# A lead of four tiles and a mean turned by transposing DMA, in a graph, attention and expert layer on one core

## What is computed

```python
deg = max(segment_sum(ones, dst), 1)
xn = layernorm(x)
agg = segment_sum(xn[src], dst) / deg[:, None]          # the mean over incoming edges
x = x + xn @ W1.T + b1 + agg @ W2.T + b2                # graph part
      + attention(xn)                                   # linear attention, 16 heads
x = x + experts(layernorm(x))                           # two chosen experts of eight
```

## Time and profile before

| | us |
|---|---|
| median of 3 executions | 1580.96 (1580.53 to 1581.2) |
| the profiled execution | 1580.07 |
| its span, first to last instruction | 1578.3 |
| TensorE busy | 1519.8 (96%) |
| VectorE, ScalarE, GpSimd busy | 1003.1, 604.5, 799.0 |
| first pass | up to about 325 |
| layers | about 350 to 1295 |
| experts | behind that |

### The profile page before, as it was taken

The page is one execution under the profiler, slowest core; times in us unless marked ns, Lnnn a source line. Parts: engine busy times, 40 slices in busy tenths (PEclk is TensorE's granted clock), DMA queues, the critical chain, the costliest instruction groups (busy, mean ns, idle before and its releaser), DMA issues.

```text
span 1578.3 us, 29172 instructions
## 1 busy us (share of the span) xinstructions
PE 1519.8 (96%) x7597; PEld 733.7 (46%) x7598; DVE 1003.1 (64%) x2154; ACT 604.5 (38%) x997; POOL 799.0 (51%) x847
## 2 busy tenths in 40 slices
PE   5999999989999999999999999999999989999997
PEld 2444444444544444444444444444544444444443
DVE  7576522246666667666677666666666666666777
ACT  5777721111333333332333333333333335555554
POOL 4122143646777767777767777767777710000000
PEclk8999999999999999999999999999999989999998
DMA  9977776957777767777767777767777723322323
GB/s 237 262 170 190 189 179 132 217 151 208 234 235 234 234 209 231 234 234 237 233 206 239 239 240 233 234 209 236 236 233 233 233 80 120 107 90 96 106 87 112
DMA packets 166610, 308.64 MB, mean 196 GB/s; under 512 B 71986, under 2 KB 74572, under 8 KB 166260
## 3 DMA queue, kind: packets, MB, share of 16 engines
q0 software_dynamic: 62720, 205.57, 44.3%
q1 hardware_dynamic: 36112, 58.90, 11.7%
q10 hardware_dynamic: 67684, 42.96, 10.7%
HBM read 255.02 MB, written 39.49 MB: 187 GB/s over the span
## 4 chain that ended last, share of the span: by engine, by line
PE 70%; POOL 14%; issue 6%; DVE 3%; DMA 1%; ACT 0%; DVEq 0%; SPq 0%; ACTq 0%
POOL ring L522 14%; PE bank L549 13%; PE bank L554 13%; PE bank L550 12%; PE bank L622 8%; PE bank L623 8%; PE bank L708 2%; PE bank L709 2%; PE bank L710 2%; PE bank L742 2%; PE bank L747 2%; PE bank L743 2%; PE bank L793 1%; PE bank L838 1%; PE bank L800 1%
## 5 line engine op out<-in xcount | busy, mean ns | idle before, releaser
L522 POOL DMA_INDIRECT ring<-table,src_col x784 | 753.5, 961 | 328.9 <-issue 254.5
L622 PE MATMUL bank<-ring,onehot 128*128 x830 | 316.1, 381 | 14.8 <-issue 6.2
L623 PE MATMUL bank<-ring,onehot 128*128 x830 | 315.5, 380 | 0.0
L1238 DVE TENSOR_TENSOR onehot<-bank,dst_col 128x512 f32 x244 | 168.8, 692 | 96.5 <-issue 61.1
L961 ACT ACTIVATE work<-bank,rd 128x512 f32<-128x512 f32 x49 | 33.7, 687 | 336.4 <-DVE rd L1271 336.3
L549 PE MATMUL bank<-wts,xT 128*128 128x512 f16 x392 | 149.1, 380 | 4.1 <-DVE wts L1313 4.1
L550 PE MATMUL bank<-wts,xT 128*128 128x512 f16 x392 | 149.0, 380 | 0.0
L549 PE MATMUL bank<-wts,work 128*128 128x512 f16 x392 | 148.2, 378 | 0.2 <-DVE work L1441 0.2
L550 PE MATMUL bank<-wts,work 128*128 128x512 f16 x392 | 148.3, 378 | 0.0
L622 PEld LDWEIGHTS bank<-ring,onehot 128*128 x830 | 80.9, 97 | 126.5 <-issue 45.6
L623 PEld LDWEIGHTS bank<-ring,onehot 128*128 x830 | 81.1, 98 | 84.8 <-issue 0.9
(11 more groups left out here) (284 smaller groups left out, 2732.5 us busy)
## 6 DMA issues: line engine op xcount, KB each, us to landing
ring<-table,src_col POOLq DMA_INDIRECT x784, 3.7
x_rows<-work ACTq DMA_DIRECT2D x49, 256.0 KB, 3.7
work<-in_x ACTq DMA_DIRECT2D x48, 256.0 KB, 4.3
ring<-x_rows SPq DMA_DIRECT2D x12, 1024.0 KB, 5.3
out_x<-ring SPq DMA_DIRECT2D x12, 1024.0 KB
table<-xT SPq DMA_DIRECT2D x45, 256.0 KB, 3.5
ring<-in_x SPq DMA_DIRECT2D x42, 256.0 KB, 3.7
xT<-in_L_mix_qkv_weight SPq DMA_DIRECT2D x2, 1024.0 KB, 10.1
```

Of the source, the lines that this page charges most:

```text
L522: pool.indirect_dma_start(ring[:, n, :], None, table[:, :], bass.IndirectOffsetOnAxis(ap=ap, axis=0)).then_inc(slot_loaded[n], 16)
L622: mm(ps_agg[:, :], w[:, k, :], rows[:, k, 0:D], start=start, stop=False, skip_group_check=True)
L623: r = mm(ps_agg[:, :], w[:, k, :], rows[:, k, D:2 * D], start=False, stop=stop, skip_group_check=True)
L1238: V.tensor_tensor(onehot[:, bass.ds((q + t) % OG * U, U), :], ps_iota[:, None, :].to_broadcast([P, U, P]), dst_col[:, bass.ds(q % GROUPS * ...
```

## The change

The lead of the aggregation goes from three tiles to four (`SKEW`), the mean's buffers from four to five, and there is one more early tile, in step 36 of the first pass. The empty layers are 14, 25, 36 and 47. The mean is kept as 16-bit halves side by side: ScalarE writes the high half out of the bank, VectorE the low half (`low_ah`), which now empties the bank. ScalarE issues a transposing DMA of both halves (`turn_ah`), which replaces TensorE's four transposes, ScalarE's L1056 and VectorE's L1441. VectorE's sums of x2 move from the head of the next layer to the end of the layer: degrees, sums, low half, and then the one-hots of the next layer.

```diff
-SKEW = 3
+SKEW = 4
-SLOTS = 4
-EARLY = {39: 0, 42: 1, 45: 2}
-LAYERS = ((1, 4, 3), (4, 12, 3), (12, 13, None), (13, 24, 2), (24, 25, None), (25, 36, 1), (36, 37, None), (37, T, 0),
-          (T, T + 3, None))
+SLOTS = 5
+EARLY = {36: 0, 39: 1, 42: 2, 45: 3}
+LAYERS = ((1, 4, 4), (4, 14, 4), (14, 15, None), (15, 25, 3), (25, 26, None), (26, 36, 2), (36, 37, None), (37, 47, 1),
+          (47, 48, None), (48, T, 0), (T, T + 3, None))
...
-        ah = work[:, 7:7 + SLOTS]
+        ah = work[:, 7:7 + SLOTS].rearrange("p k f -> p (k f)").bitcast(F16).rearrange("p (k f) -> p k f", k=SLOTS)
...
# TensorE, layer
-                    after(pe, s["ah_made"], t + 1)
-                    after(pe, s["ahT_lo"], t)
...
-                    for c in range(C):
-                        r = nc.tensor.transpose(ps_ta[:, c * P:(c + 1) * P], ah[:, (k - 1) % SLOTS, c * P:(c + 1) * P], ident[:])
-                    r.then_inc(s["turned_ah"], 1)
...
-                    after(pe, s["ahT_lo"], t + 1)
+                    after(pe, s["ah_turned"], 16 * t + 16)
...
# ScalarE
             def keep_ah(t, k):
 
                 act.wait_ge(s["rd_made"], t + 1)
-                after(act, s["turned_ah"], t - SLOTS + 1)
-                F(ah[:, k % SLOTS, :], ps_agg[:, :], ACT.Copy, scale=rd[:]).then_inc(s["ah_made"], 1)
+                after(act, s["ah_turned"], 16 * t - 16 * SLOTS + 16)
+                F(ah[:, k % SLOTS, 0:D], ps_agg[:, :], ACT.Copy, scale=rd[:]).then_inc(s["ah_hi"], 1)
+
+            def turn_ah(t, k):
+
+                after(act, s["ah_made"], t + 1)
+                after(act, s["w2_used"], t)
+                act.sem_inc(s["act_turn"], 1)
+                act.dma_start_transpose(ahT.rearrange("p a c n -> p (a c) n"), ah[:, k % SLOTS, :]
+                                        ).then_inc(s["ah_turned"], 16)
...
             keep_ah(SKEW, SKEW)
+            turn_ah(0, 0)
...
                 if skew is not None:
                     keep_ah(i + skew, k + skew)
+                t = i
+                if real(t):
+                    turn_ah(t, k)
...
# VectorE
+            def low_ah(t, k):
+
+                after(dve, s["ah_hi"], t + 1)
+                V.scalar_tensor_tensor(out=ah[:, k % SLOTS, D:2 * D], in0=ps_agg[:, :], scalar=rd[:],
+                                       in1=ah[:, k % SLOTS, 0:D], op0=ALU.mult, op1=ALU.subtract).then_inc(s["ah_made"], 1)
...
                     degrees(i + skew)
+                t = i - 1
+                if real(t):
+                    end = isinstance(t, int) and t == T - 1
+                    after(dve, s["lin_made"], t + 1)
+                    after(dve, s["x2_stored"], 16 * t)
...
+                    V.scalar_tensor_tensor(out=x2, in0=ps_b[:, :], scalar=mix[:, 2:3], in1=x2,
+                                           op0=ALU.mult, op1=ALU.add).then_inc(s["x2_made"], 1)
+                if skew is not None:
+                    low_ah(i + skew, k + skew)
             layers(dve, layer)
```

More of the change, by code:

```diff
@@ L121, in layers @@
     for lo, hi, skew in LAYERS:
[L122 to L125, removed]
-            body(i, skew, i % SLOTS)
[L127 to L132, removed]
+        n = (hi - lo) // SLOTS
+        if n > 1:
+            with eng.Fori(0, n) as g:
+                for k in range(SLOTS):
+                    body(g * SLOTS + lo + k, skew, (lo + k) % SLOTS)
+            lo += n * SLOTS
+        for i in range(lo, hi):
+            body(i, skew, i % SLOTS)
 def program(nc, x, src, dst, gw1, gb1, gw2, gb2, qkv_w, proj_w, proj_b, attn_w, attn_b, gate_w, gate_b,
@@ L194, in program @@
         x2, xn2, acc, pT_, x_in, w32, ahT_ = (work[:, k] for k in range(7))
-        ah = work[:, 7:7 + SLOTS]
-        x_end = ah[:, (T - SLOTS) % SLOTS]
+        ah = work[:, 7:7 + SLOTS].rearrange("p k f -> p (k f)").bitcast(F16).rearrange("p (k f) -> p k f", k=SLOTS)
+        x_end = work[:, 7 + (T - 4) % SLOTS]
         ahT, pT = (v.bitcast(F16).rearrange("p (a c n) -> p a c n", a=2, c=C) for v in (ahT_, pT_))
@@ L308, in natural @@
                 return xT[:, t + OFF].rearrange("p a n -> p (a n)")
-            return (ksb[:, :], work[:, 10], work[:, 11], awb[:, :])[t - (T - NS)].bitcast(F16)
+            return (work[:, 10], ksb[:, :], work[:, 11], awb[:, :])[t - (T - NS)].bitcast(F16)
         def stored(eng, t):
@@ L817, in layer @@
                 if real(t):
-                    after(pe, s["ahT_lo"], t + 1)
+                    after(pe, s["ah_turned"], 16 * t + 16)
                     three(ps_o[:, :], lambda c: ahT[:, 0, c, :], lambda c: ahT[:, 1, c, :],
-                          lambda c: wg2[:, 0, c, :], lambda c: wg2[:, 1, c, :], C, first=False)
+                          lambda c: wg2[:, 0, c, :], lambda c: wg2[:, 1, c, :], C, first=False).then_inc(s["w2_used"], 1)
                 if ahead is not None:
@@ L1016, in _ @@
                 if i - 2 in EARLY:
+                    if EARLY[i - 2] == SKEW - 1:
+                        stored(act, T - NS)
                     keep_ah(EARLY[i - 2], EARLY[i - 2])
@@ L1343, in _ @@
                     degrees(EARLY[i - 2])
+                    low_ah(EARLY[i - 2], EARLY[i - 2])
                 if i + 1 in EARLY:
@@ L1360, in _ @@
             dve.wait_ge(s["ksum_made"], 1)
-            stored(dve, T - NS)
+            stored(dve, T - NS + 1)
             link(V.tensor_scalar(ksb[:], bank[4][:, :], mix[:, 0:1], None, ALU.mult))
@@ L1400, in _ @@
             degrees(SKEW)
+            low_ah(SKEW, SKEW)
             for j in range(C):
@@ L1409, in layer @@
             def layer(i, skew, k):
[L1410 to L1423, removed]
                 if skew is not None:
@@ L1495, in layer @@
                     degrees(i + skew)
+                t = i - 1
[3 more added lines that the diff above has]
+                    after(dve, s["x2_stored"], 16 * t)
+                    if end:
+                        dve.wait_ge(s["x_end_loaded"], 16 * len(parts(TAIL)))
+                    else:
+                        after(dve, s["x_loaded2"], 16 * t + 16)
+                    V.scalar_tensor_tensor(out=x2, in0=ps_o[:, :], scalar=mix[:, 1:2], in1=x_end if end else x_in,
+                                           op0=ALU.mult, op1=ALU.add).then_inc(s["sum_steps"], 1)
+                    after(dve, s["sum_steps"], 2 * t + 1)
+                    V.scalar_tensor_tensor(out=x2, in0=ps_b[:, :], scalar=mix[:, 2:3], in1=x2,
+                                           op0=ALU.mult, op1=ALU.add).then_inc(s["x2_made"], 1)
+                if skew is not None:
+                    low_ah(i + skew, k + skew)
             layers(dve, layer)
```

13 lines of the change are left out of this document (5 added, 8 removed).

## The result

Four runs of each kernel gave 1616.1 us (1610.86 to 1619.38) after and 1581.08 (1580.53 to 1583.27) before; the ratio is 1.0216, interval 1.0194 to 1.0238. The direction was forecast, the size was not: 1585.8 was the prediction, 1595 its upper end. Most of the 35 us comes from two things of which the forecast's sum has no term. The profiled execution took 1617.16 us, its span 1615.3.

What follows compares the result with a forecast made beforehand. The prediction took GpSimd's gather, with its spacing and eight stops, to bound the layer loop. Its terms, -2.0 + 0.9 + 3.5 + 2.4 = +4.8 us, against a median of 1580.96 gave 1585.8 us, range 1578 to 1595.

Steps and rivals of the forecast that it cites:

- The gather as the bound, 1.264 us a block: Layer loop: GpSimd's gather needs 20.2 us per tile of 16 blocks, whatever TensorE does, and with its stops places the end.
- rival (c): Layer loop: transposes slow the gather by 0.02 us on some 690 blocks, 13 us, giving 1596.9 us; chance 0.05.
- The lead of four: First pass: one more early tile puts the gather 11.5 us ahead, 12.8 with three stops shortened by 0.43 each.
- The lead is spent by a fourth layer without aggregation: End of the layer loop: empty layer 47 uses up the lead, so the last degrees come only 2.0 us sooner.
- the forecast's 8.0: First pass: the extra early tile costs TensorE 8.0 us, so everything behind the first pass comes that much later.
- block 96: First slot after the boundary of the first pass: gathered at 370.9 us, where before this block came at 382.4.
- What would show it: List of signs; its last: query ends 2.6 us into each layer, low half some 2.4, leaving 0.2 us of room.
- the terms of +4.8: Whole kernel: loop end -2.0, one-hots +0.9, transposes in empty layers +3.5 and tail +2.4 make it 4.8 us slower.
- three stops of some 5.4: Gather's ring full behind the first three empty layers: 5.4 us each, plus what the transpose adds.
- One-hots behind an empty layer, +0.9: Behind empty layers TensorE waits 0.1 to 1.5 us for VectorE's one-hots; 0.9 taken, counting only after the fourth.
- transposes in empty layers, +3.5: Four empty layers: transposing DMAs land on average 0.88 us beyond their 5.5 us cover, 3.5 in all, bounds 0 to 12.
- The tail, +2.4: Behind the last degrees: sums, low half, transposing DMA and 24 matmuls take 12.9 us instead of 10.5.

Runs made afterwards that it cites:

- e8: The kernel before with only the lead of four (TensorE still transposes the mean) and its loops over layers written out: 1583.8 us, ratio 1.0008.
- e6: The changed kernel with its loops over five layers written out, nothing else: 1608.6 us, ratio 1.0175.
- e5: The changed kernel with two aggregation banks used in turn and its layer loops written out: 1591.6 us, ratio 1.0074.
- e7: The kernel before with one wait added: ScalarE's eviction of the mean waits for the second sum, freeing the aggregation's bank late: 1620.1 us, ratio 1.0238.
- e3: The changed kernel with the schedule of before (lead of three, four buffers, loops of four layers): 1604.2 us, ratio 1.0148.
- e4: e3 with the aggregation alternating between two banks by the tile's parity: 1592.2 us, ratio 1.0061.
- e13: The kernel before with its loops over four layers written out: 1581.1 us, ratio 1.0000.
- e2: The kernel before with the lead of four alone, loops as in the changed kernel, mean still turned by TensorE: 1589.5 us, ratio 1.0058.
- e11: The kernel before with its loops over four layers written out, in a round where the kernel before took 1824.6 us: 1791.7 us.
- e10: The kernel before with its loops over four layers written out, in a round where the kernel before took 1822.9 us: 1794.4 us.

## Why the prediction was right or wrong, point by point

**The gather as the bound, 1.264 us a block: right for before, but not what bounds after.** The spacing did not change (0.96 and the pause of 0.29 above), so rival (c) is out. But the fall of GpSimd's share of the chain to 2% and the 49.1 us of full ring say that the bound moved.

**The lead of four: right.** Without the loops' events (e8) tile 47's degrees came at 1250.26; the forecast, less the 1.3 us of the turning, was 1248.1. The first stop was 8.61, with 7.5 named. "The lead is spent by a fourth layer without aggregation" is what e8 shows: 1583.8 against 1582.0. One cost ahead of the layers was missing, though. The first query of the layers starts at 334.56 in e8, 7.5 us later than before (327.06), near the forecast's 8.0; but at 338.49 in after, 336.48 in e6 and 337.85 in e5. Of that, 2.1 us in after are waits for one-hots between 229 and 328 us, where e8 has none. The low halves of the four early tiles are the likely reason, which no run tests. With the boundary's wait as forecast (5.85 for 5.07 + 0.75), block 96 came at 374.53 instead of 370.9.

**The step that failed** is the overlap of the low half with the query, in the last line of "What would show it": "query ends 2.6 us after the layer's start, the low half some 2.4: 0.2 us of room, which costs only where the gather isn't behind". It is wrong in three ways.
- The room was measured to the end of the query. TensorE's sequencer needs it earlier: 687.75 - 686.86 = 0.89 us lie between the end of the low half and the first block. Room was -0.6, not +0.2.
- The price is not 0.6 but 1.1 us, as the next starts are ragged too (e5 against after, row by row; e7 gives 1.05).
- "Only where the gather isn't behind" took TensorE's slack for free. It should have been 20.2 - 18.83 = 1.4 us a layer, and became 20.2 - 19.94 = 0.26. With 1.4 TensorE soon works off what the gather got ahead in an empty layer: in e5 layers 15 to 19 take 18.5 to 18.9 us and layer 20 already 21.1. With 0.26 it doesn't: in after layers 15 to 24 take 19.6 to 20.3, all but layer 20. The ring stays full, and each disturbance stops the gather: at 649 us for 6.6, at 748 and 757 for 7.1, at 871 for 13.7, at 1084 for 8.6 us, where three stops of some 5.4 were forecast. Up to 1285 us the stops sum to 49.1 us in after, 37.4 in e6 and 25.1 in e5.

The price in the time: 16.3 us (e6 against e5), or 12.6 with the lead of three (e3 against e4). That the kernel became slower was forecast for other reasons, the terms of +4.8, so of its direction that much is luck.

**A step that was missing: the loops.** The forecast moved the layers' borders and never asked where the loops now end: 8.4 us (after against e6), of which layer 20's loop-back is 5.6 in the traces.

**One-hots behind an empty layer, +0.9; transposes in empty layers, +3.5.** Behind the last empty layer TensorE waits 0.92 us for one-hots in e5, and in after, where it comes later, not at all. Layers 14 and 36 of after took 11.23 us, untouched. Layer 25 took 866.69 - 850.39 = 16.30 and waited 3.57; layer 47 took 13.5. Over 11.23 that is 7.3 us in four layers, twice my mean and within the 0 to 12 of the bounds. But in e6, with the late bank and without loops, the same two excesses are 1.0 and 0.2, and in e5 nought, so most of it is gone when the loops are; one execution of each can't tell that from chance. e4 and e3 have one late transpose each in their three empty layers, both in layer 36 (15.5 and 12.85 us). In e4's, ScalarE's issue of it took 2.52 us, about twice the usual, and VectorE's sequencer stood 3.9 us behind its loop's branch (1038.0) at the same time. What makes one late lies open.

The page of the Trainium skill on Advanced Engine Details and Errata, X-Bar Transpose (TRN2), has transposing DMAs as fast as regular ones. In layers 14 and 36 of after and in all four empty layers of e5 TensorE waited for it 0.2 us at most. In layer 25 of after, 9.0 us from issue to use, and in layer 36 of e4, 7.9 us, it does not hold for a transpose beside the gather; the 256 KB store of the same queue, a regular one, landed in 3.7 before.

**The tail, +2.4: right.** From the last degrees to the end of the span it is 1615.3 - 1312.26 = 303.0 us after and 1578.3 - 1277.58 = 300.7 before: +2.3. e5 gives 1586.7 - 1283.65 = 303.0 again; e8, which has TensorE's transposes, 1582.5 - 1280.60 = 301.9, so against that it is 1.1.

**The whole**, by experiments: the lead 1.8 (e8), the loops 8.4 (after to e6), the bank 16.3 (e6 to e5), which leaves 8.5 us between e5 and e8 for the turning and VectorE's order without the bank wait. Together the 35, each step known to some 4 to 6 us either way. The profiled executions of e5 and e8 differ by only 4.2 us (1586.7 against 1582.5), and these can be placed: e5's layers begin 3.3 us later (above), its first layer takes 30.12 us against 26.04, the tail is 1.1 longer, and the layers between them give 4.3 back. In the first layer TensorE waits twice for one-hots in e5 (7.1 us in all, against one wait of 5.1), the second time behind the first low half and the matrix's split, which VectorE now does ahead of them; behind each wait the granted clock is 0.5 for a while, so twice in e5 and once in e8. The other 4 us of the 8.5 lie between executions and are not placed. The forecast, 1585.8, knew neither the late bank nor the loops; e5, which has neither, took 1591.6. The late begin and the first layer, for which the sum had only 0.75, are more than this difference.

No version here beats the kernel before; e8 and e13 equal it within their intervals.

## What to carry to other kernels

When a change makes a second engine the last reader of a buffer that another engine's queue waits for, don't compare the two ends; add what the waiting sequencer has yet to do behind the wait, here 0.9 us. Work taken from an engine that isn't the bound is its slack, and slack is what drains the queue of the engine that is: write down its amount per round before and after. And where a schedule's borders move, list where each engine's loops turn.

## What the runs showed of the hardware

- A wait at the head of a group costs TensorE more than its length. In e7 the bank came free 2.5 us into the layer, when the query was just ending (2.6); the first block started at 3.40 instead of 2.59, and the layer was 1.05 us longer.
- At single loop-backs VectorE's sequencer ran nothing for 5.2 us behind the branch (after, 745 us) and 4.0 us (e2, 520 and 735 us), and for 2.65 us behind the exits of after's loops; 0.05 to 0.31 us in the kernel before, which gains nothing when all of its loops are written out (e13).
- After the waits of 4.3 and 3.6 us (after, at 753 and 859 us) and of 7.3 us (e2, at 531 us) TensorE went on at a granted clock of 0.5, which is 1.2 GHz: 0.60 to 0.61 us for a matmul of 0.38.
- In the rounds with 1823 us for the kernel before, a hand-over between engines is slow. In e11 the last matmul of an aggregation starts at 726.96 and VectorE's degrees at 730.23, 3.3 us later, waiting for a releaser that the profile calls remote; in the trace of before it is 0.25 (802.32 to 802.57). Between 400 and 1400 us the profile has 32 such waits of VectorE's degrees. There written-out loops were worth 1.5 to 2%. Whether this belongs to a chip is open: the record gives e10 (1822.9 us for the kernel before) and e13 (1581.6), ten minutes apart, the same chip number. That a change counts for nothing has to be said with the time of before from the same round beside it.

```profile
726.96 0.19 PE L610 MATMUL bank<-ones,zero 128*128 128x1 f16 x2
...
730.23 0.16 DVE L1268 TENSOR_SCALAR dg<-bank 128x1 f32<-128x1 f32 x1 [6.21 <-remote]
...
DVE dg L1268 <- remote: 217.9, 32, 10.9
```
